# One Mamba and expert layer over 16 sequences: z tiles projected ahead of x tiles, the next tokens' norm moved forward, a product ahead of the square sums, and the slot places moved to the end

## What is computed

```python
h = _L0_tok_ref(A, B, x, log_dt, 512)                 # state-space kernel: 64 token rows of 512 per sequence
h = concatenate([h, softmax(table)[x_txt]], axis=1)   # 128 text rows more: (16, 192, 512)
h = h + attn(layernorm(h))
h = h + moe(layernorm(h))

def attn(x):                                          # D_INNER 1024, 16 heads of 64, state 64
    zxbcdt = einsum('btd,pd->btp', x, W_in)           # z, x, B, C, dt
    dt = softplus(dt + dt_bias)
    xBC = silu(causal_conv(xBC, 4 taps))
    y = scan(h*exp(dt*A) + dt*B*x ; y = h*C) + D*xh
    y = y * silu(z)
    y = y * rsqrt(mean(y*y) + RMS_EPS) * norm_w
    return einsum('bti,di->btd', y, W_out)

def moe(x):                                           # 32 experts, top 8, of which 4 may be rerouted
    probs = softmax(x @ gate.T); top, idx = top_k(probs, 8)
    ... the similarity of secondary to primary experts reroutes some of them ...
    for each expert: y += (silu(g)*u) @ wd.T * weight
```

## Time and profile before

| | us |
|---|---|
| runs before | 2018.80, 2026.16, 2029.17 (median 2026.16) |
| the profiled execution | 2018.31 |
| its span | 2016.6 |
| PE busy | 1632.1 (81%) |
| DVE busy | 977.5 (48%) |
| POOL busy | 770.4 (38%) |
| ACT busy | 696.4 (35%) |

### The profile page before, as it was taken

How to read it: one execution, slowest core, us unless ns; L and a number is a source line. 1 busy time by engine, 2 the same in 40 slices (tenths; PEclk the granted TensorE clock), 3 DMA queues, 4 the chain that set the end, 5 groups by cost and what they waited for, 6 DMA issues and landing times. The chain is left out here.

```text
span 2016.6 us, 29775 instructions
## 1 busy us (share of the span) xinstructions
PE 1632.1 (81%) x8741; PEld 1122.7 (56%) x8742; DVE 977.5 (48%) x2238; ACT 696.4 (35%) x1456; POOL 770.4 (38%) x635
## 2 busy tenths in 40 slices
PE   7999999965978878787878630588888888888896
PEld 7999999753655646465565320344444444444443
DVE  5464545244468777877877451133333333333332
ACT  2533434225726455462635000122222222222221
POOL 5211100000312474565547654243444444444443
PEclk9999999876889889888988565799999999999999
DMA  7010000041432232343331020566665666666644
GB/s 277 27 53 12 1 12 1 17 168 51 134 99 89 85 93 80 95 150 93 91 85 43 2 48 0 151 136 153 143 134 132 134 155 140 136 139 152 162 87 85
DMA packets 92310, 193.81 MB, mean 96 GB/s; under 512 B 34472, under 2 KB 42960, under 8 KB 87489
## 3 DMA queue, kind: packets, MB, share of 16 engines
q0 software_dynamic: 36464, 86.90, 19.7%
q1 hardware_dynamic: 55760, 105.78, 17.4%
HBM read 143.31 MB, written 49.32 MB: 96 GB/s over the span
## 5 line engine op out<-in xcount | busy, mean ns | idle before, releaser
L1810 PE MATMUL moe_ps_gu<-moe_wgu,moe_xt 128*128 x944 | 336.7, 500 | 60.4 <-issue 42.8
L1702 POOL DMA_INDIRECT out_h<-moe_yy,moe_idx_s x119 | 188.2, 1582 | 381.3 <-DVE moe_yy L1775 208.8
L1810 PEld LDWEIGHTS moe_ps_gu<-moe_wgu,moe_xt 128*128 128x128 f32 x944 | 171.0, 191 | 180.3 <-issue 87.2
L961 POOL DMA_INDIRECT scratch_slots<-lay_toki,lay_slot x192 | 219.7, 1144 | 60.8 <-issue 55.0
L1800 PE MATMUL moe_ps_y<-moe_wd,moe_ht 96*128 x476 | 229.0, 603 | 14.6 <-issue 12.5
L1738 ACT ACTIVATE moe_sl<-moe_ps_gu 128x192 f32<-128x192 f32 x118 | 39.1, 331 | 500.0 <-PE moe_ps_gu L1810 500.0
L1109 PE MATMUL lay_ring<-lay_xnt,win_sb 128*128 128x128 f32 (+2 forms) x1152 | 179.1, 306 | 28.5 <-DVE lay_xa L1315 23.1
L1182 PE MATMUL lay_ring<-head_wout,lay_yb 128*128 128x512 f32 x384 | 187.1, 645 | 0.0
L1109 PEld LDWEIGHTS lay_ring<-lay_xnt,win_sb 128*128 128x128 f32 (+2 forms) x1152 | 160.5, 209 | 37.8 <-DVE lay_xa L1315 25.1
L1770 DVE SCALAR_TENSOR_TENSOR moe_hh<-moe_sl,moe_cwv,moe_ps_gu 128x192 f32<-128x192 f32 x118 | 48.9, 414 | 221.2 <-ACT moe_sl L1738 221.2
L1315 DVE SCALAR_TENSOR_TENSOR lay_xa<-lay_ring,head_cw,lay_xa 128x378 f32<-128x378 f32 (+5 forms) x240 | 141.7, 609 | 25.9 <-ACT lay_xa L1013 20.2
(11 more groups left out here) (287 smaller groups left out, 2699.5 us busy)
## 6 DMA issues: line engine op xcount, KB each, us to landing
lay_m<-scratch_cum SPq DMA_DIRECT2D x16, 1536.0 KB, 7.4
moe_wgu<-in_wgu SPq DMA_DIRECT2D x32, 768.0 KB, 5.1
moe_wd<-in_wd SPq DMA_DIRECT2D x32, 384.0 KB, 6.8
scratch_xg<-lay_x SPq DMA_DIRECT2D x48, 136.0 KB
out_h<-lay_hres SPq DMA_DIRECT2D x48, 128.0 KB, 2.4
win_sb<-in_win SPq DMA_DIRECT2D x1, 4384.0 KB, 16.1
tok_u_raw<-in_tok_u SPq DMA_DIRECT2D x16, 256.0 KB, 4.2
tok_v_raw<-in_tok_v SPq DMA_DIRECT2D x16, 256.0 KB, 4.7
```

Of the source, the lines that this page charges most:

```text
L961: pool.indirect_dma_start(out=a["slots"], out_offset=bass.IndirectOffsetOnAxis(ap=slot[:, j, k:k + 1], axis=0), in_=toki[:, j:j + 1], in_o ...
L1702: pool.indirect_dma_start(out=a["out"], out_offset=bass.IndirectOffsetOnAxis(ap=idx_s[n][:, 0:1], axis=0), in_=yy[n][:], in_offset=None, b ...
L1810: last = mm(ps_gu[n][:], xt[n][:, t], wgu[:, bass.ds(r * KD + t, 1)].rearrange("p o n -> p (o n)"), start=t == 0, stop=t == KD - 1)
```

## The change

It moves instructions in `build_layer` and adds or removes none of the work.

```diff
-XZ_ORDER = [("x", k) for k in range(4)] + [(c, k + (4 if c == "x" else 0)) for k in range(4) for c in "zx"] + \
-    [("z", k) for k in range(4, MI)]
+XZ_ORDER = [("z", k) for k in range(MI)] + [("x", k) for k in range(MI)]
...
                 def project_text(i):
                     if i:
-                        pool.wait_ge(ring_pe, made("z", i - 1, MI - 1))
+                        pool.wait_ge(ring_pe, made("x", i - 1, MI - 1))
...  (POOL)
                         gate_y(i, 1)
+                    if pairs(n + 1):
+                        norm_tokens(n + 1)
                     if late:
                         fill_lists(8, 12)
...
-                    if pairs(n + 1):
-                        norm_tokens(n + 1)
                     if pairs(r):
                         list_places(r)
...  (PE)
                     if pairs(i):
+                        output(i, 0)
                         square_columns(i)
-                        output(i, 0)
...  (DVE)
                             skip(i, q)
+                    if pairs(n + 1):
+                        new_tokens(n + 1)
                     if pairs(r):
                         router_choices(r)
+                    if pairs(n + 1):
+                        norm_tokens(n + 1)
                     if pairs(n):
                         step_columns(n)
...
                     if pairs(i):
                         residual(i, 1)
-                    if pairs(r):
-                        router_places(r)
-                    if pairs(i):
                         residual(i, 2)
-                    if pairs(n + 1):
-                        new_tokens(n + 1)
...
                         state_matrix(n, 1)
-                    if pairs(n + 1):
-                        norm_tokens(n + 1)
+                    if pairs(r):
+                        router_places(r)
```

## The result

| | before | changed |
|---|---|---|
| median of the runs, us | 2021.06 (2013.96 to 2029.17) | 2016.26 (2008.47 to 2021.52) |
| ratio to before, 95% interval | | 0.9968 [0.9954, 0.9982] |
| span of the profiled execution | 2016.6 | 2008.4 |
| mean granted clock of TensorE over it | 0.905 | 0.888 |

Forecast was 1970, with 1930 to 1996 as the range. The change gains 0.3%, some 5 to 8 us, where 53 were expected. The two spans differ by 8.2 us, so the question is where the other 45 went.

A forecast was written before the change was run, and what follows sets the result against it. In the layer stage no engine is near full: a DVE-to-PE cycle of 88.3 us bounds it. Savings of 5.0+15.3+18.8+21.6 less 2.9 and 4.6 give 53 us, a forecast median of 1970, range 1930 to 1996.

The forecast's parts named there:

- The tail: Iteration's end, paced by DVE: norm and places leave the path, so it shrinks from 36.5 to 23.2 us.
- S to T: From the square columns' first DVE instruction (S) to PE's next opening transposes of normed token rows (T); forecast 23.2 us.
- Iteration 0: Iteration without routing, its last products PE-bound: 72.1 for 87.4 us, saves 15.3.
- The layer's end: Last pair's lists start later behind the moved places, and their fills delay DVE: costs 4.6 us.
- Iteration -1: Before the first full layer work: next opening in effect at 478.8 for 483.75, held by ACT's copy; saves 5.0 us.
- The head: T to S: PE waits some 5 us for a bank, then y tiles at half clock; grows from 51.7 to 60.3 us.
- Iteration 1: No places precede it, so DVE is early and the clock stays up: 70.1 for 88.9 us, saves 18.8.
- The granted clock: PE in the y tiles: falls to half behind the bank wait and stays there, 2.49 us a tile against 1.47.
- Rival A: Clock stays up over the 5 us stall: 7.3 us more saved in iterations 2 to 6, 1932 us; chance 0.14.
- rival C: Half clock from y tiles on, z, x and block 0 not restoring it: iteration 107, 2085 us; chance 0.04.
- Rival B: Clock falls more often, also before block 2 and around T: 15 to 20 us less saved, 1988; chance 0.20.
- The statistics beside the gate: Norm statistics on DVE during POOL's gate: one input, not held, cost 0; if held, 1.1 us.

The follow-up runs named there:

- e1_copies_first: The changed kernel with ACT copying the routed rows (x2t) ahead of the exponential of the steps; 1964.5 us, ratio to before 0.9735.
- e4_norm_alone: The kernel before with only new_tokens and norm_tokens moved forward; 2041.3 us, ratio to before 1.0071.
- e8_split_places: The changed kernel with ACT's copies first and router_places split, most of it run behind the next iteration's last skip for five pairs; 1955.8 us, ratio to before 0.9638.
- e10_split_late_hots: e8_split_places with the one-hots' transposes behind the eleventh tile and the similarities behind the fifteenth; 1933.1 us, ratio to before 0.9553.
- e2_places_back: The changed kernel with DVE counting the places behind residual 1 again; 2013.1 us, ratio to before 0.9965.
- e6_copies_and_places: The changed kernel with ACT's copies first and the places back behind residual 1; 1949.1 us, ratio to before 0.966.

## Why the prediction was wrong, step by step

- **The tail, right.** S to T is 994.91-971.80 = 23.1 us, forecast 23.2; before, 36.5. Each of its DVE steps came at its old duration.
- **Iteration 0, right.** 71.7 us, forecast as 72.1, counted from 475.6, 1.2 us ahead of ACT's copy. **The layer's end, right:** 4.7 for 4.6. Iteration -1 saved 7.5 for 5.0, partly because the decays began earlier.
- **The head, the step that failed.** "Behind the places are queued steps (1.4), two skips (1.4) and the convolution of the first bc tile": this list follows DVE's queue to one consumer, the bank, and stops. It doesn't ask which other engine waits for the steps, and what stands behind that wait in its queue. ACT waits for them (L1044) with the copies of x2t behind, and PE needs the first copy one product earlier than the bank. The bank was free at about T+16.2 (918.36 and half of 3.68), as forecast (T+16.4). PE's wait ended with the copy instead, at T+16.1; that the two fall together is luck. Its start was T+7.5 for T+11.3. So six products instead of five, two transposes and two more logits ran behind it at half clock: the last product ends at T+38.1 for T+30.8, and S at T+67.8 for T+60.3. That is 7.5 us in each full iteration, and in `e1_copies_first` S is back at T+60.5. A small slip beside it: from tail and head 13.3-8.6 = 4.7 us are saved per iteration, not 5.4, which sets the new 83.5 against a mean of 88.9 where the cycle added up came to 88.3.
- **Iteration 1, wrong for the same cause.** "The clock stays up": DVE is early there, but its steps still come 3.78 us after PE wants the copy, and the granted clock of 562 to 580 is 0.50. It took 85.6 us for 70.1; with the copies first it took 70.0. These 15.5 us, 4 x 7.0 in iterations 2 to 5 and 6.8 in iteration 6 make 50.3; less the 2.5 that iteration -1 saved beyond the forecast and the 2.0 of the experts, they are the 45 missed, to 1 us.
- **The granted clock, right in kind.** Forecast: "once low, y products do not bring it back". So it was, here and in `e1_copies_first` and `e4_norm_alone`, where the stretches behind the wait (883 to 898, 935 to 945) were granted 0.50 as well. Rival A (clock stays up over a 5 us stall) and rival C (half clock through z, x and block 0) did not occur: three z tiles take 2.07, 1.92 and 1.69 us, the next 1.06. Rival B had the right sign, and its half clock in iteration 1's y tiles did occur, but for another reason: the waits that it named, before block 2 and at the opening, did no harm. Block 2 takes 7.11 us in iterations 2 to 5, and the first bc tile of the iteration at 903.96 takes 1.10 us, both full clock.
- **Nearly no gain had 3% of the chances.** The head's growth was priced from one wait. Rival C named the point of no change, some 5 us more per iteration. The 7.0 us more of iterations 2 to 5 went past it, by what stands behind the earlier wait inside the y tiles; I had looked for it only beyond them.
- **The statistics beside the gate cost nothing**, as taken. In the changed kernel they ran from 942.80 for 0.69 us while the gate began at 943.04; the multiply of two SBUF inputs behind them was held. The Trainium skill (GPSIMD Engine Reference, Key points) says that GpSimd collides with VectorE's instructions of two SBUF inputs or in a 2-port mode; the trace agrees for the multiply (2.29 us) and for the add in `e8_split_places` (3.31 us). The same rule, applied to the add beforehand, would have told where not to put it.

## What to carry to other kernels

When an instruction is made late on one engine, list every engine that waits for its result, and for each what is queued behind that wait; a copy that has nothing to do with the late value can be what the bottleneck engine needs next. When a wait of PE moves, price the stretch that follows it at half clock: 3.87 us of idle ahead of projections cost two tiles of 1.97 and 1.71 for 1.06 us, 1.27 to 3.80 us ahead of state products had all of them that followed at half clock. Where a wait can't be removed, independent tiles ahead of it can keep both the time and the clock, as they did behind the choices in `e10_split_late_hots`.

## What the runs showed of the hardware

- Once it had fallen inside the state products, the granted clock stayed at 0.50 for as long as they (64 columns by 192 and 64 by 64) lasted, with PE busy all of the 17.0 us of 921 to 938. Two to three projections later it was at full.
- A wait of 1.27 us inside the state products (`e2_places_back`) was followed by half clock for the rest of them; without it (`e6_copies_and_places`) they kept the full clock in five of six iterations, worth 12 us each (89.0 against 77.2 to 77.8). In other places 1.09 us of waiting passed without harm.
- Adding 8 us of products that nobody needs per iteration made the kernel 3% faster than the changed one (1952.9 for 2016.3).
- The clock can fall in state products with no wait in front: 0.95 from 628 to 639 and 0.51 from 639 to 650 in `e10_split_late_hots`, PE 11.00 of 11.00 us busy in both. The same products kept the clock in its iterations 1 and 3 to 6. What decides is open.
- An add of 128x32 bf16 on DVE took 3.31 us beside a GpSimd multiply of two SBUF inputs, for 0.17.
